# First stage's recurrence with the channel on the partitions: head pairs in two column halves, decayed C, skip on VectorE

## The reference, cut to what matters

```python
zxbcdt = x @ W_in
z, xBC, dt = jnp.split(zxbcdt, [512, 512 + 640], axis=-1)
xBC = jax.nn.silu(causal_conv4(xBC))
xh, B, C = jnp.split(xBC, [512, 576], axis=-1)        # C, B: 64 columns
dt = jax.nn.softplus(dt + dt_bias)
a = cumsum(dt * A)                                     # per head, in a chunk
Y = (C B^T * exp(a_l - a_s) * causal) @ (xh * dt)      # inside the chunk
  + exp(a_l) * (C @ state)                             # from the chunks before
  + xh * D                                             # skip
state = exp(a_end) * state + (B * exp(a_end - a_s))^T @ (xh * dt)
Y = Y * jax.nn.silu(z)
Y = Y * jax.lax.rsqrt(jnp.mean(Y * Y, -1) + EPS) * norm_w
x = x + Y @ W_out @ W_lin + b_lin
```

## Time and profile before

| | us |
|---|---|
| median of three runs | 2358.94 (2358.38 to 2359.93) |
| the profiled execution | 2360.41 |
| its span, first to last instruction | 2358.5 |
| TensorE busy | 2189.1 (93%) |
| VectorE busy | 1803.0 (76%) |
| ScalarE busy | 1566.7 (66%) |
| GpSimd busy | 1146.6 (49%) |

### The profile page before, as it was taken

How to read it: one execution, slowest core, us unless ns; L and a number is a source line. 1 busy time by engine, 2 the same in 40 slices (tenths; PEclk the granted TensorE clock), 3 DMA queues, 4 the chain that set the end, 5 groups by cost and what they waited for, 6 DMA issues and landing times.

```text
span 2358.5 us, 26231 instructions
## 1 busy us (share of the span) xinstructions
PE 2189.1 (93%) x8900; PEld 1393.1 (59%) x8900; DVE 1803.0 (76%) x2083; ACT 1566.7 (66%) x2541; POOL 1146.6 (49%) x928
## 2 busy tenths in 40 slices
PE   7999999999999999989999999998999987787998
PEld 4544545555555556456766666676766664444886
DVE  5666767777777765324999998999989998996665
ACT  5577686777686845425676767677676868775444
POOL 2101322222231313213988888888988888890000
PEclk9999999999999999999999999999999999898999
DMA  6243332323232323233323232323323221312121
GB/s 234 72 134 102 108 116 90 125 96 122 87 125 88 119 90 134 83 107 109 131 93 125 90 125 89 117 99 107 117 100 125 90 83 43 117 36 98 36 81 45
DMA packets 117495, 241.22 MB, mean 102 GB/s; under 512 B 8770, under 2 KB 66370, under 8 KB 116978
## 3 DMA queue, kind: packets, MB, share of 16 engines
q1 hardware_dynamic: 108290, 207.14, 26.4%
q0 software_dynamic: 8528, 31.36, 3.8%
q10 hardware_dynamic: 544, 1.05, 0.1%
HBM read 219.20 MB, written 20.32 MB: 102 GB/s over the span
## 4 chain that ended last, share of the span: by engine, by line
PE 65%; ACT 10%; POOL 10%; DVE 10%; issue 5%; DMA 0%; ACTq 0%; DVEq 0%; POOLq 0%
PE ps L685 13%; PE ps L727 10%; POOL dB L2306 6%; PE ps L971 5%; DVE h L1473 3%; PE ps L849 2%; PE ps L823 2%; PE ps L955 2%; POOL acc L2288 2%; PE ps L709 2%; ACT ps L1659 2%; ACT L1657 1%; POOL du L2302 1%; PE ps L755 1%; PE ps L753 1%
## 5 line engine op out<-in xcount | busy, mean ns | idle before, releaser
L1473 DVE TENSOR_TENSOR_SCAN h<-ps,hst,dB 128x512 f32<-128x512 f32 x512 | 636.9, 1270 | 59.0 <-ACT ps L1659 50.5
L2306 POOL TENSOR_TENSOR dB<-du,bc 128x512 f32<-128x512 f32 x512 | 648.0, 1287 | 61.6 <-DVE h L1473 59.1
L685 PE MATMUL ps<-wgt,msg 128*128 128x512 f32 x1024 | 489.0, 598 | 2.1 <-DVE xb L1181 2.1
L1659 ACT ACTIVATE ps<-dt,cols 128x512 f32<-128x512 f32 x512 | 351.9, 692 | 181.1 <-DVE h L1473 178.8
L727 PE MATMUL ps<-raw,msg 128*128 128x256 f32 x1792 | 436.3, 379 | 0.9 <-ACT hb L1659 0.9
L971 PE MATMUL ps<-consts,h 128*128 128x128 f32 x2048 | 318.9, 281 | 70.7 <-DVE acc L1435 38.0
L971 PEld LDWEIGHTS ps<-consts,h 128*128 128x128 f32 x2048 | 251.6, 144 | 224.8 <-DVE acc L1435 73.4
L727 PEld LDWEIGHTS ps<-raw,msg 128*128 128x128 f32 x1792 | 324.0, 190 | 74.1 <-issue 42.1
L685 PEld LDWEIGHTS ps<-wgt,msg 128*128 128x128 f32 x1024 | 190.0, 192 | 206.2 <-issue 204.6
L1659 ACT ACTIVATE wgt<-wgt 128x1024 f32<-128x1024 f32 x256 | 257.9, 1046 | 51.9 <-DVE wgt L1146 50.5
L2288 POOL TENSOR_TENSOR acc<-acc,part 128x512 f32<-128x512 f32 x174 | 226.4, 1301 | 59.7 <-ACT part L1659 58.3
(11 more groups left out here) (320 smaller groups left out, 3589.9 us busy)
## 6 DMA issues: line engine op xcount, KB each, us to landing
raw<-in_adjT SPq DMA_DIRECT2D x256, 512.0 KB, 3.4
bc<-tmp_bc SPq DMA_DIRECT2D x64, 512.0 KB, 4.6
E<-tmp_bc POOLq DMA_DIRECT2D x32, 512.0 KB, 4.1
xb<-in_xT POOLq DMA_DIRECT2D x8, 512.0 KB, 4.1
tmp_x<-xb POOLq DMA_DIRECT2D x8, 512.0 KB, 4.2
x<-tmp_x SPq DMA_DIRECT2D x8, 512.0 KB, 5.8
tmp_x<-x SPq DMA_DIRECT2D x8, 512.0 KB, 4.8
msg<-in_W SPq DMA_DIRECT2D x4, 1024.0 KB, 10.6
```

Of the source, the lines that this page charges most:

```text
L685: x = e.matmul(P[d][:, :], msg[:, j, d * 128:(d + 1) * 128], wgt[g % NW][:, l, :], start=j == 0, stop=j == NJ - 1)
L1473: e.tensor_tensor_scan(hr[n % 3][:, m, :], PS[4 + k % 2].t[:, :], dBr[k % 4][:, :], hst[:, n % 16, m:m + 1], ALU.mult, ALU.add).then_inc(S ...
L1659: return e.activation(out, in_, func, bias=bias, scale=scale)
L2306: e.tensor_tensor(dBr[k % 4][:, :], du[:, m, :], bcr[i % 3][:, n % 2, :], ALU.mult).then_inc(S("dB"), 1)
```

## The change

The recurrence's output now has channels on the partitions and rows along the free axis. In `outer(s)`, for every head, `xdt`'s 64 columns are stationary and `E` (128 columns) is moving; even heads write the partitions 0 to 63 of bank `Y`, odd heads 64 to 127, and two heads share 128 columns. The part of the state goes into the same bank first: C is multiplied by exp(a) beforehand (`cs`: two Exp on ScalarE out of the raw sums in `E`, then a multiply on GpSimd), the state's 64 columns are stationary. The state has its heads 0 to 3 on partitions 0 to 63 and 4 to 7 on 64 to 127, the other quarters are zero, and `St` is two matmuls of 256 columns. The skip is a multiply-add on VectorE while it evacuates `Y`. `inner(s)` stays as it is. All of `outer(s)` on TensorE stands in one lump after three empty steps.

z is made with channels on the partitions, so nothing is turned back: the 16 transposes, `YT` and the row scaling are gone. The squares are summed by GpSimd (`squares`) into `sqs`, one matmul with a matrix of 1/256 gives the mean over the channels, and VectorE multiplies the product with `Wc` by its inverse root. `ssd_ring` has 25 uses in a block instead of 32, `NSA` is 59 instead of 62.

```diff
 # outer(s), TensorE
-                    e.matmul(Yo.ps[:, :], cc[:, 5, ts_], h0[:, :], start=True, stop=True).then_inc(Yo.full, 1)
...
-                    e.matmul(St.ps[:, :], bn[:, :], xdec[:, :], start=True, stop=True).then_inc(St.full, 1)
...
-                    for m in range(4):
-                        e.matmul(Y.ps[:, m * 128:(m + 1) * 128], cc[:, m, ts_], diagD[:, m, :], start=m == 0, stop=False,
...
+                    def place(h):
+                        return Y.ps[64 * (h % 2):64 * (h % 2) + 64, h // 2 * 128:h // 2 * 128 + 128]
...
+                    w.wait_ge(S("cs"), 4 * ib + s + 1)
                     w.wait_ge(S("M"), 4 * ib + s + 1)
                     w.wait_ge(X.evac, X.n)
...
                     for h in range(8):
-                        i = e.matmul(Y.ps[:, h * 64:(h + 1) * 64], Es[:, h, :], xd[:, h * 64:(h + 1) * 64], start=False,
-                                     stop=h == 7, skip_group_check=True)
+                        e.matmul(place(h), h0[:, h * 64:(h + 1) * 64], cs[:, h % 4 * 128:h % 4 * 128 + 128], start=h < 2,
+                                 stop=False, skip_group_check=True)
+                    for g in range(2):
+                        i = e.matmul(St.ps[64 * g:64 * g + 64, 0:256], bn[:, :], xdec[:, 256 * g:256 * g + 256],
+                                     start=True, stop=True)
+                    i.then_inc(St.full, 1)
+                    for h in range(8):
+                        i = e.matmul(place(h), xd[:, h * 64:(h + 1) * 64], Es[:, h, :], start=False, stop=h >= 6,
+                                     skip_group_check=True)
                     i.then_inc(Y.full, 1)
...
 # outer(s), VectorE
-                    e.tensor_tensor(heads(tmp[:, :]), heads(Yo.ps[:, :]), ecd[:, 0, s, :, None].broadcast_to([128, 8, 64]),
-                                    ALU.mult).then_inc(Yo.evac, 1)
...
-                    e.tensor_tensor(h0[0:64, :], hd[:, :], St.ps[0:64, :], ALU.add).then_inc(St.evac, 1)
+                    for g in range(2):
+                        i = e.tensor_tensor(half_state(h0, g, 256 * g), half_state(hd, g, 256 * g), half_state(St.ps, g), ALU.add)
...
-                    e.tensor_tensor(tmp[:, :], tmp[:, :], Y.ps[:, :], ALU.add).then_inc(Y.evac, 1)
+                    w.wait_ge(S("sqs"), 2 * (c - 1))
+                    for m in range(4):
+                        ms_ = slice(m * 128, (m + 1) * 128)
+                        i = e.scalar_tensor_tensor(x[:, ms_], cc[:, m, ts_], col("D0", m), Y.ps[:, ms_], ALU.mult, ALU.add)
...
 # end of ssd, VectorE
+                    e.tensor_tensor(tmps[m][:, :], b.ps[:, :], sqs[:, :], ALU.mult).then_inc(S("y2"), 1)
...
 # inner(s), ScalarE
+                    for g in range(2):
+                        act(css[c % 2][64 * g:64 * g + 64, :], E[c % 3][64 * g:64 * g + 64, 4 * g:4 * g + 4, :].rearrange("p h l -> p (h l)"),
+                            ACT.Exp).then_inc(S("E"), 1)
...
 # end of ssd, ScalarE
-                act(rms[:, :], ms[:, :], ACT.Ln, scale=1.0 / 512, bias=EPS).then_inc(S("rms"), 1)
...
-                    act(YT[:, :, s * 128:(s + 1) * 128], b.ps[:, :].rearrange("p (m l) -> p m l", m=4), ACT.Identity).then_inc(b.evac, 1)
+                act(b.ps[:, :], b.ps[:, :], ACT.Ln, scale=256.0 / 512, bias=EPS).then_inc(S("rms"), 1)
...
+                act(sqs[:, :], b.ps[:, :], ACT.Exp, scale=-0.5).then_inc(b.evac, 1)
...
 # inner(s) and outer(s), GpSimd
+                    e.tensor_tensor(quad, quad, ccs[p][:, 5, None, s * 128:(s + 1) * 128].broadcast_to([128, 4, 128]),
+                                    ALU.mult).then_inc(S("cs"), 1)
...
+                    e.tensor_tensor(x[:, 0:256], x[:, 0:256], x[:, 256:512], ALU.add).then_inc(S("sqs"), 1)
...
+                    e.tensor_tensor(sqs[:, s * 128:(s + 1) * 128], x[:, 0:128], x[:, 128:256], ALU.add).then_inc(S("sqs"), 1)
```

More of the change, by code:

```diff
@@ L852, in ssd @@
                         yield
-                v = ssd_use(ib, 27)
-                yield from norm_a(tmp[:, :], z[:, 2, :], ssd_use(ib, 26), v, (S("xsum2"), ib + 1), (S("sqsum2"), ib + 1))
+                    if m == 0:
+                        b = ssd_use(ib, 16)
+                        w.wait_ge(S("sqs"), 8 * ib + 8)
+                        w.wait_ge(b.evac, b.n - 1)
+                        e.matmul(b.ps[:, :], avg, sqs[:, :], start=True, stop=True).then_inc(b.full, 1)
+                        yield
+                v = ssd_use(ib, 20)
+                yield from norm_a(tmp[:, :], z[:, 2, :], ssd_use(ib, 19), v, (S("xsum2"), ib + 1), (S("sqsum2"), ib + 1))
                 w.wait_ge(v.evac, v.n)
@@ L2218, in ssd @@
                     yield from outer(s)
+                squares(3)
                 if ib + 2 < NB:
-                    w.wait_ge(S("hd"), 4 * ib + 4)
+                    w.wait_ge(S("sqs"), 8 * ib + 8)
                     halves(ib + 2)
-                yield from [None] * 13
-                x2 = [ssd_use(ib, 24 + m) for m in range(2)]
+                yield from [None] * 10
+                x2 = [ssd_use(ib, 17 + m) for m in range(2)]
                 for b in x2:
```

221 lines of the change are left out of this document (104 added, 117 removed).

## The result

The changed kernel takes 2381.52 us (median of four runs, 2380.58 to 2385.01), the kernel before in the same session 2359.43 (2358.38 to 2360.60, four runs): a ratio of 1.0096, 95% interval 1.0079 to 1.0114. The forecast was 2305 with a range of 2280 to 2362. It has the wrong sign, and the time is outside the range.

A forecast was written before the change was run, and what follows sets the result against it. TensorE was taken to bound blocks 0 to 5: -9.7 work, +1.3 switch, +1.0 waits, -7.4 us each, -44 in six; blocks 6 and 7 add -10. Together -54 from 2360.4 gives 2306, adjusted to 2305 us; range 2280 to 2362.

The forecast's parts named there:

- TensorE's work: TensorE, per block: 19.4 us removed, 8.9 + 0.9 added with overlapped halves, so -9.7 us; in series -0.8.
- the overlap of the halves: TensorE's lump: even and odd heads' column halves run at once, 2.22 us a chunk instead of 4.45; chance 0.57 as summed.
- The switch: TensorE changing between full width and halves, 8 times a block: 0.16 us each, 1.3 us a block (0 to 2.0).
- ScalarE and VectorE's added work: Per block: ScalarE +4.2 us to 88.2; VectorE 83.1 instead of 83.7, its evacuation behind the lump 2.7 us.
- the new waits: TensorE waiting at the lump's head for state, xdec, cs, E, or ahead of Wc: 1 us a block (0 to 3).
- -7.4: Blocks 0 to 5, change per block in us: -9.7 work + 1.3 switch + 1.0 waits; six blocks -44.
- ScalarE's slack: ScalarE in regular blocks: its 88.2 us of busy time were taken to fit in a block of 105 us.
- The other engines take over: Rival: ScalarE's order sets regular blocks at 88.2 + 14.2 + 7 = 109.4 us, 3.0 less; 2335 us, chance 0.15.
- Blocks 6 and 7: Last two blocks, little product to hide the chunk chain: -5 us each (0 to -8.4), -10 together.
- The signs that I named: Trace of after: lump records every 0.055 us, blocks near 105 us, TensorE's waits under 4, VectorE's seven operations 2.7, ScalarE 88.
- The one sign that was to prove the prediction wrong outright: TensorE's lump: a record still every 0.11 us would make the prediction wrong outright.
- my three: Rivals: other engines take over, 2335 us (0.15); serial halves without drain, 2353 (0.13); serial with drain, 2371 to 2377 (0.15).

The follow-up runs named there:

- e7: Changed kernel with GpSimd's cs multiply cut to 16 columns and its first add of squares to 8, the rest left out; 2379.85 us (one run).
- e8: Changed kernel with three chunks' squares later on ScalarE, first z evacuation sooner, GpSimd's hd ahead of the next multiply of E; 2334.45 us, 0.9894.
- e9: Kernel before with the two Exp per chunk for cs added on ScalarE, into a scratch tile nothing reads; 2381.49 us (one run).
- e6: Changed kernel with GpSimd's hd (decay of the state) ahead of the next chunk's multiply of E; 2378.05 us (one run).
- e5: Changed kernel with ScalarE's evacuation of the first z tile sooner in its order; 2380.96 us (one run).
- e3: Changed kernel with ScalarE's first square of a block moved behind a pair of wgt operations and an evacuation; 2362.44 us, 1.0018.
- e13: Kernel before with its first square later on ScalarE, z evacuation sooner and GpSimd's hd ahead of the multiply of E; 2358.98 us, 1.000.
- e1: Changed kernel with heads in the order 0,2,4,6,1,3,5,7, so four matmuls in a row use one column half; 2390.05 us, 1.0142.
- e2: Changed kernel without ScalarE's two Exp per chunk for cs; GpSimd multiplies the conv's tiles instead; 2362.32 us, 1.0023.

## Why the prediction was wrong, point by point

**TensorE's work: right.** This and the next point compare block 2. The lump took 2.33 us (forecast 2.2), a record each 0.058 us (0.055), the work at the higher clock 101.4 us (101.75). What I had called decisive, the overlap of the halves, came out. The switch costs 0.1 us a side, where 0.16 was taken.

**ScalarE and VectorE's added work: right as work.** ScalarE was busy 88.0 us (88.2), the seven operations took 2.66 (2.7). VectorE as a whole was wrong, 90.0 instead of 83.1; GpSimd's work beside it explains 4.6 us of that (e7), and GpSimd had 41.7 us, not 35.

**The failed step: "I put the new waits at 1 us a block (0 to 3)".** They were 7.6 us (9.86 of idleness after, 2.23 before), and behind them 4.8 us were lost at the lower clock, for which the sum had no term. 7.6 + 4.8 instead of 1.0 is 11.4 us more; -7.4 + 11.4 = 4.0, less 0.35 by which the work was better than forecast, gives the +3.7 that was measured. I looked for these waits at the lump's head and ahead of `Wc`. They came at L756 and L863, of which the prediction doesn't speak: I followed the instructions that were changed, and not those that stand behind them in ScalarE's and VectorE's order and free TensorE's banks. The part at L756, 5.3 + 2.0 us, runs through ScalarE's order, and the moves of e8 take it away. The part at L863, 2.5 us more than before and 2.8 at the lower clock, goes with a pair of `wgt` operations in VectorE's order by the rows; no run has removed it.

**The step under it: ScalarE's slack.** "ScalarE's 88.2 us fit in 105" goes by busy time. Its idle time was no slack, since most of it stayed when work was added. e9 shows it without any of the change's layout: 5.1 us of ScalarE work cost 2.0 to 3.0 us a block.

**The rival was right in kind.** *The other engines take over* had the mechanism, 88.2 busy plus ScalarE's waits, and a chance of 0.15. Its sum was 88.2 + 14.2 + 7 = 109.4. Measured: 88.0 + 13.7 + 14.4 = 116.1, which as a sum of busy and idle time must come out; what tells is that neither kind of idle time shrank. I had let half of the other 14 us go, and they stayed whole. With them the rival would have read 116.4 and been the one on the slower side. The argument against it, that TensorE now makes its output sooner, failed on VectorE: in block 2 L1210 waits 2.3 us for ScalarE's `sm`, which two `cs` pairs delay, and the output's operations stand behind it.

**Blocks 6 and 7: -5 each forecast, -0.2 and about +3 measured.** The chain there runs over GpSimd's `hd`, which I had given "most of a chunk to spare". Once it goes first (e6, one run) 5 us come back, and with all moves blocks 6 and 7 and what follows give 9.5 of the 10 forecast.

**The signs that I named.** The record distance, VectorE's 2.7 us and ScalarE's 88 came as said; block distance and TensorE's waits did not. The one sign that was to prove the prediction wrong outright, a record every 0.11 us, didn't come either, and it was wrong all the same. The overlap was the wrong thing to make the rivals of: two of my three were about it.

## What to carry to other kernels

Idle time of an engine that runs a fixed order isn't slack: before adding work, ask of each of its waits whether it would shrink, and of each instruction behind the added one who waits for it, above all evacuations that free another engine's buffer. When a wait is the longest in the list, take it away alone before believing it: in e5 it was gone and the block the same, while moving a wait on the engine that closes the loop (e3) gave 4 us a block. Time an order change together with the layout that needs it: moves of this kind were worth 47 us after the change (e8), and three of them nothing before it (e13).

## What the runs showed of the hardware

- Matmuls of 64 stationary columns on the two column halves overlap down to 0.058 us a float32 record of 128 columns, and still mostly (2.93 us for the lump) when four heads of one half come in a row.
- In e1 records of `St` (L824) start before the last state matmuls (L821) that stand ahead of them in the program and use the other half: 475.22 against 475.55 us. With the halves alternating no such rows appear (after, block 2).
- A switch between full width and halves cost about 0.1 us.
- Waits of 5.3 and 3.5 us in an otherwise busy TensorE were followed by stretches at the lower clock that cost 2.0 and 2.8 us; the granted clock was at 1.2 GHz already before work went on (0.50 in 492 to 493). From 225 us to the end of stage A, after has 88.7 us at the lower level, before 3.4, e3 58 and e8 37.5. In e8 such a stretch also comes at 457, where the wait shortly before is only 1.05 us long (454.54).
- GpSimd's work beside VectorE stretched VectorE's: 7.1 us less of the one made the other's unchanged work 4.6 us shorter (e7). A pair of L1153 took 5.40 us in e2, and 2.35 at the same place before.
